# Three-sublayer decoder layer: every engine's order of steps written out as word lists instead of computed from slot tables, with three more waits

## What is computed

```
x = layernorm(x + attention(x))    # 16 heads of 16; causal; of each row only the 32 largest scores are kept,
                                   # softmax over them, times v, output projection
x = layernorm(x + experts(x))      # 8 experts: relu(proj_in[e] @ x) (256 -> 512), proj_out[e] @ h (512 -> 256),
                                   # weighted by gate[e], the sum of ctx where itok == e
x = layernorm(x + ffn(x))          # Hadamard rotation, 4-bit activations, ternary 256x256 weight
```

## Time and profile before

| | |
|---|---|
| three timed runs | 576.58, 575.6, 575.65 us (median 575.65) |
| profiled execution, first to last instruction | 574.0 us |
| busy: PE, DVE, ACT, POOL | 521.3, 457.4, 409.2, 346.6 us |
| mean granted clock of TensorE | 0.967 |
| bytes moved, mean | 24.08 MB, 42 GB/s |

### The profile page before, as it was taken

How to read it: one execution, slowest core, us unless ns; L and a number is a source line. 1 busy time by engine, 2 the same in 40 slices (tenths; PEclk the granted TensorE clock), 3 DMA queues, 4 the chain that set the end, 5 groups by cost and what they waited for, 6 DMA issues and landing times. The chain is left out here.

```text
span 574.0 us, 22290 instructions
## 1 busy us (share of the span) xinstructions
PE 521.3 (91%) x8116; PEld 443.4 (77%) x8116; DVE 457.4 (80%) x2846; ACT 409.2 (71%) x1018; POOL 346.6 (60%) x355
## 2 busy tenths in 40 slices
PE   5757659999999999999999999999999999999973
PEld 3535548888888888888888888888888888888851
DVE  2698988896988989998998889998999899504115
ACT  2888788776767687768866687768686878566641
POOL 1587485955547466755574556656565756476762
PEclk9888888999999999999999999999999999999995
DMA  7544440002000101100120102000200010000000
GB/s 228 174 150 148 126 157 18 3 2 59 3 24 18 23 3 38 40 3 21 41 58 2 23 11 67 3 22 3 76 4 22 2 39 3 1 2 19 2 14 24
DMA packets 23230, 24.08 MB, mean 42 GB/s; under 512 B 2129, under 2 KB 20049, under 8 KB 23121
## 3 DMA queue, kind: packets, MB, share of 16 engines
q1 hardware_dynamic: 23120, 22.65, 13.0%
HBM read 18.32 MB, written 2.10 MB: 36 GB/s over the span
## 5 line engine op out<-in xcount | busy, mean ns | idle before, releaser
L541 POOL TENSOR_TENSOR h_lo<-h_raw,h_hi 128x512 f16<-128x512 f32 x128 | 148.9, 1164 | 114.4 <-ACT h_raw L693 113.0
L895 PE MATMUL ps_o<-w_hi,h_lo 128*128 128x256 f16 x512 | 139.7, 273 | 3.5 <-POOL h_lo L541 3.5
L879 PE MATMUL ps_z<-x1t_hi,w_lo 128*128 128x256 f16 x512 | 140.0, 273 | 0.2 <-DVE x1t_lo L1043 0.2
L879 PE MATMUL ps_z<-x1t_lo,w_hi 128*128 128x256 f16 x512 | 139.7, 273 | 0.0
L879 PE MATMUL ps_z<-x1t_hi,w_hi 128*128 128x256 f16 x512 | 139.6, 273 | 0.0
L895 PE MATMUL ps_o<-w_hi,h_hi 128*128 128x256 f16 x512 | 139.6, 273 | 0.0
L895 PE MATMUL ps_o<-w_lo,h_hi 128*128 128x256 f16 x512 | 139.5, 273 | 0.0
L689 ACT ACTIVATE h_hi<-ps_z 128x512 f16<-128x512 f32 x128 | 76.2, 595 | 71.7 <-PE ps_z L879 71.6
L987 DVE MATCH_REPLACE8 taken<-next,taken 128x64 f32<-128x64 f32 (+4 forms) x480 | 110.7, 242 | 0.1
L562 POOL TENSOR_TENSOR acc<-go_sb,acc 128x512 f32<-128x512 f32 x55 | 70.0, 1273 | 34.3 <-ACT go_sb L703 34.2
L982 DVE MAX8 next<-taken 128x8 f32<-128x64 f32 (+4 forms) x480 | 85.5, 245 | 0.1
(11 more groups left out here) (142 smaller groups left out, 1037.3 us busy)
## 6 DMA issues: line engine op xcount, KB each, us to landing
w_raw<-in_w1t SPq DMA_DIRECT2D x8, 512.0 KB, 3.8
w_raw<-in_w2t SPq DMA_DIRECT2D x8, 512.0 KB, 3.7
v_pad<-v_sb SPq DMA_DIRECT2D x16, 136.0 KB, 2.7
xt_sb<-in_xt SPq DMA_DIRECT2D x8, 256.0 KB, 3.9
x_sb<-in_x SPq DMA_DIRECT2D x8, 256.0 KB, 3.1
xa_sb<-in_xt SPq DMA_DIRECT2D x7, 256.0 KB, 3.7
out<-out_sb SPq DMA_DIRECT2D x7, 256.0 KB, 3.8
ctx_sb<-in_ctx_w SPq DMA_DIRECT2D x8, 128.0 KB, 3.2
```

Of the source, the lines that this page charges most:

```text
L541: nc.gpsimd.tensor_tensor(h_lo[:, e % 2, 2 * z:2 * z + 2, :], h_raw[:, z, :, :], h_hi[:, e % 2, 2 * z:2 * z + 2, :], ALU.subtract)\
L879: last = pe.matmul(ps_z[z][:, d * UT:(d + 1) * UT], w[:, e, c, at:at + P], x[:, c, :], start=n == 0, stop=n == len(terms) - 1)
L895: last = pe.matmul(ps_o[e % 2][:, b * D:(b + 1) * D], h[:, e % 2, c, b * SEQ:(b + 1) * SEQ], w[:, e, c, :], start=n == 0, stop=n == len(te ...
```

## The change

The tables and the sort are gone. `ORDER` holds one string of step names for each engine; `name*3` stands for three steps in a row. The k-th time that a name stands in an engine's string, it is the k-th step of that name, by unit and then by the step's own numbers. `all_steps` lists what exists. All 477 PE steps, 429 DVE, 418 ACT, 280 POOL and 56 SP steps are the same as before. No instruction that computes or moves data is added, removed or altered.

```
-def build_schedule():
-    placed = []
-    def put(slot, engine, name, v, *args):
-        placed.append((slot, (engine, name, v, args)))
...
-    return [step for _, step in sorted(placed, key=lambda x: x[0])]
+ORDER = {
+    "pe": """
+        k q ffn_sum v scores*2 w_sum v w_sum k scores turn_probs q turn_probs k w_sum scores v turn_probs w_sum
+        v turn_probs scores attend turn_probs w_sum attend turn_probs k scores attend turn_probs*2 w_sum k v
+        attend turn_o w_sum out_proj q scores k turn_probs turn_x1 turn_probs L1 q L1 turn_probs L1*2 w_sum L1
...
+    "dve": """
+        gate_sums ffn_ternary first_max select*2 w_scale first_max select*5 keep w_scale select*7 first_max keep
...
+def all_steps():
...
+def build_schedule():
+    waiting = {}
+    for engine, name, v, *args in all_steps():
+        waiting.setdefault((engine, name), []).append((v, args))
+    waiting = {key: iter(sorted(steps)) for key, steps in waiting.items()}
+    placed = []
+    for engine, words in ORDER.items():
+        for word in words.split():
+            name, _, count = word.partition("*")
+            for _ in range(int(count or 1)):
+                v, args = next(waiting[engine, name])
+                placed.append((engine, name, v, args))
+    return placed
@@ exp on ACT
                     if n < TILES * UNITS - 1:
                         act.wait_ge(s_copied, n + 2)
+                    else:
+                        act.wait_ge(p_ready, n)
@@ x1t_high, x2t_high on ACT
                     act.wait_ge(ready, v + 1)
+                    if name == "x1t_high":
+                        wait(act, l1_done, RING_STEPS * v)
@@ gate_sums on DVE
                     dve.wait_ge(s_ctx, 32 * (v + 1))
+                    wait(dve, gate_ready, v)
```

More of the change, by code:

```diff
@@ L105, in expert_steps @@
     return steps + [("L2", EXPERTS - 1, 0), ("L2", EXPERTS - 1, 1)]
[L108 to L147, removed]
[3 rows of a table removed]
-    "gated_add": 2.5, "quantise": 85.5, "load_x": -14.5, "gate_scale": 48.75, "store": 102.75, "move_v": 10.25,
-    "q": -11.5, "load_ctx": 29.75, "gate_out": 0.5, "x1t_low": 43.75,
-}
@@ L155 @@
-FINAL = STEADY | {
-    "hadamard": 86.75, "copy_q4t": 99, "ffn": 130.5, "ffn_residual": 97.5, "ffn_scale": 97.25, "turn_q4": 99.75,
-    "to_q4": 86.75, "gate_out": -15, "quantise": 87.5, "out_proj": 59, "move_v": -4.25, "v": 98.5, "gate_sums": 31.5,
-    "turn_o": 38.25, "x2t_high": 80.25, "experts": 51.25, "keep": 4.5, "copy_probs": 2.5, "copy_q": -12,
-    "load_x": -18.25, "copy_k": -13, "rstd3": 97.5, "x1t_high": 52.25, "rstd2": 79, "load_xt": -25.25, "shift1": 2,
-    "turn_x1": 44, "x2t_low": 82.75, "normalise": 6.5, "x_plus_bo": 22, "x1t_low": 53.25, "shift0": 10, "attend": 5,
-    "gate_scale": 59, "h_low": -2.5, "turn_probs": 0.25, "turn_x2": 81.75, "select": 8, "spread_q": -11.75,
-    "copy_probs2": 4, "load_ctx": 26.5, "k": 75.25, "shift2": 2, "gated_add": 4, "copy_scores": -8.25, "relu": -2,
-    "pace": 1.25, "q": -9, "copy_v": 121.25, "scores": -5.5, "store": 105, "ln2_apply": 81.5, "shift3": 0.75,
-    "ln1_stats": 38, "rstd1": 39.5, "ln1_apply": 38.5, "turn_probs2": 8.25, "copy_ot": 36.75,
-}
@@ L220, in build_schedule @@
+def all_steps():
+    for v in range(UNITS):
+        for kind, e, z in expert_steps():
+            yield "pe", kind, v, e, z
+            if kind == "L1":
+                yield "act", "relu", v, e, z
+                yield "pool", "h_low", v, e, z
+            elif z == 1 and not (v == SPLIT and e == EXPERTS - 1):
+                yield "act", "gate_out", v, e
+                yield "pool", "gated_add", v, e
         for k in range(TILES):
-            tile = base + SLOTS // TILES * k + at[f"shift{k}"]
@@ L230, in build_schedule @@
-            put(base + at["spread_q"] + k, "pool", "spread_q", v, k)
+                yield engine, name, v, k
+            for half in range(2):
+                yield "pe", "turn_probs", v, k, half
+                yield "act", "copy_probs", v, k, half
         for b in range(UB):
-            put(base + at["gate_sums"] + b, "dve", "gate_sums", v, b)
+            yield "dve", "gate_sums", v, b
+            if v == SPLIT:
+                yield "dve", "gated_last", v, b
         for engine, name in UNIT_STEPS:
-            if v == 0 or (engine, name) not in AHEAD_STEPS:
-                put(base + at[name], engine, name, v)
+            yield engine, name, v
```

153 lines of the change are left out of this document (114 added, 39 removed), and 3 rows, old and new, of the table LAST.

## The result

| | before | after |
|---|---|---|
| timed runs | 575.6 to 576.58, median 575.64 us (4) | 565.56, 567.73, 569.25, 571.48, median 568.49 us (4) |
| ratio, with its 95% interval | | 0.9882 [0.9842, 0.9921] |
| profiled execution, span | 574.0 us | 563.7 us (its run: 565.56) |

The new order is 1.2% faster here; 570.0 was forecast. The four runs of the kernel after lie 6 us apart, and the profiled one is the fastest of them. So its rows alone would show too much. The same kernel was timed and profiled a second time, beside the experiments; there it is 0.7% faster (571.06 us).

A forecast was written before the change was run, and what follows sets the result against it. PE was taken as the bound from the first `L1`, before a fixed tail: 574.0 - 3.8 + 1.3 - 3.5 + 0.4 = 568.4 us span, plus 1.65 gives 570.0 us. Range 563 to 581; the forecast's own 566.5 to 573.

The forecast's parts named there:

- Projections, -3.8: `q2` and `k5` on PE fill the layernorm gap behind `out_proj0`, ahead of the first `L1`: 3.8 us gained.
- First `L1`, +1.3: `v0` ahead of the scores and changed DVE work start the first `L1` 1.3 us later, at 90.0; range -1 to +5.
- if the first `L1` lies beyond 93: Sign in the profile after: a first expert step on PE beyond 93 us would make the prediction wrong.
- Other marks: Profile signs: first scores near 18.3, `first_max` 20.4, `norm0.3` 76, PE busy over 98.5% from 100 to 500 us.
- `h_low`, -3.5: PE's waits for `h_low` between `L1` and `L2` vanish, since at least two steps separate them: 3.5 us, ends 2.0 and 3.5.
- Other waits, +0.4: PE waits 0.4 us more at `turn_x1(1)`; the remaining 4 us of waits arise anew. Ends -4 and +20.
- Three waits, 0: Added waits for `l1_done`, `gate_scale` and `keep` on ACT and DVE cost 0; bounds -0.1 and +1.5 us.
- tail, 0: The serial chain after the last `L2`, 17.6 us of layernorm, quantisation and ffn, keeps its order: 0 change.
- The rivals: The first: PE waits on ps_misc for `normalise` at 28 `attend`, 0.55 us each, 585 us; lower forms 577 to 581; chance 0.23.
- The late first scores are not made good: DVE keeps its 5.4 us of idle time and `L1` starts 4.4 us later still: 574.4 us; chance 0.12.
- the rule weighed: Idle gaps halve PE's clock; filling one spares `turn_x1(0)` and the first `L1` some 0.5 us, left out of the sum.
- `gate_sums`: On DVE, moving eight instructions away from POOL work saves 416 against 280 ns each by the shared-port rule; sum unchanged.

## Why the prediction was right, and where its sizes were off

The forecast was -5.6 us on the span, in four terms. The total held: 568.49 us and 571.06 us lie on either side of 570.0. That it came so near is in part luck. The forecast was -6.9 us behind the first `L1` and +1.3 ahead of it; the two profiles have -9.0 and -10.4 behind it, and -1.3 and +5.8 ahead.

*Projections, -3.8.* PE has 3.9 us less to do in the stretch in the first profile, and 5.5 less in the second (459.5 to 454.1). The difference is the clock again, 2.19 against 1.32 us for the first `L1` and 2.70 against 1.89 for `q3`; that the first agrees with 3.8 to 0.1 is luck, and some 1.4 us of the 5.5 are not accounted for. The term as the prediction put it, two projections that hide under the layernorm's 4.1 us, nearly holds at full clock, where they held `turn_x1(0)` 1.0 us. At the lower one `out_proj0` and `q2` took 7.5 us together instead of 4.0, and the first `L1` came late. The prediction priced that at 1 to 2 us "if one of them runs at the low clock" and left it out of the sum, while in the kernel timed again it happened. Undoing this part alone costs 5.2 us, the whole gain, though only some 3.9 of the 8.4 us in the stretch are the projections themselves. In the old lists the move was worth nothing: there the load for `q2` came too late, a condition that the prediction does not name and that the new list of SP meets.

*First `L1`, +1.3.* Measured -1.3 in the first profile and +5.8 in the second; by the spans of the timed runs +3 to +5 is usual (an estimate, as worked out above). The step that said `v0` delays the scores to 18.3 and `first_max` to 20.4 failed in its working: it took `v0` at 3.21 us and started it at 15.02. It took 1.99 us in both profiles and started at 13.34 in the first, because `q0` ran in 1.99 as well, and at 15.06 in the second. The scores came at 15.26 and 16.98, `first_max` at 17.37 and 19.07. The prediction also took `ffn_ternary` as worth nothing, since nothing waited for it in its old place; in the new list it stands ahead of the first `max`, and with the scores put first it alone held that `max` (17.58). DVE's own stretch was sized well as a whole: 76.0 - 20.4 = 55.6 us forecast, 56.12 and 57.86 measured, with 53.4 us of work (forecast 54.6) and 2.7 and 4.4 idle (forecast 1.0). What was missing is mainly the clock. The prediction read 0.86 in the earlier trace rows as a given of the kernel, when it moved between 0.91 and 0.79 in two executions of the new order, whose PE steps now lie on the path. One of its own marks says so: "if the first `L1` lies beyond 93" it would be wrong, and in one of the two profiles it lies at 94.47. Other marks held: PE busy 99.4% from 100 to 500 us, no wait for `normalise`, two projections in the gap, 0.5 us of waits for `h_low`. Those for the first scores, `first_max` and `norm0.3` (73.49 and 76.93 for 76) did not.

*`h_low`, -3.5.* Measured -3.0 by the list of waits (3.5 to 0.5); done alone, -2.9 in the stretch and some 2 in the time. The count behind it was off a little. Written out, 14 pairs of the old order have one expert step between, not 13. The new order isn't free of them either: four pairs have one, with three or more other steps beside it in three of them and two in the fourth.

*Other waits, +0.4.* Measured -2.0: idle time of PE went down by 5.0 us, 3.0 of which are `h_low`. The waits for `keep` (1.4), `quantise` (1.1) and `normalise` (0.7) of the earlier trace rows and of the same list went, a new one for `copy_probs` (0.9) came. The prediction had assumed that as much would arise anew, without a row for it.

*Three waits, 0, and tail, 0.* Both as put: 1.0000 [0.9983, 1.0016] and 17.3 us.

*The rivals.* PE did not wait for `normalise` in the kernel after. Its place was right, and with `normalise` two stages later its time is 581.9, between the 577 and the 585 that the prediction gave. Its form was off: seven waits of 1.4 us on the mean, not 28 of 0.55. Against it stood what the prediction said, two or more steps of PE behind most `attend`; with a margin of about 1 us the chance of 0.23 was a fair one. "The late first scores are not made good" (574.4) names a late start that did occur (94.47 in the second profile), with 4.4 us of DVE idle time in place of 5.4, but for another reason, mainly the clock.

Two points stay open. The stretch of the kernel after is 9 to 10 us shorter than before, and the two parts that were tried in the old order make 4.9 of it. The rest is presumably in the order of the later units, of which no part was isolated. And why one execution of the same lists gets 0.91 and another 0.79 was not found; `q0`, the second step, already differs (1.99 and 3.78 us, behind the same 0.93 us of idle time).

On the rule weighed (the Trainium skill, "TensorE: Matmul & The Clock Gate", section "HAM oscillation — how this bites in real kernels"): the two projections did spare `turn_x1(0)` (0.66 us instead of 1.09 for the same four matmuls), but not always the first `L1`. In the first profile it started behind 1.43 us of idle time, three of its matmuls took 0.27 to 0.28 us, and the last eight 0.42 each:

```profile
89.37 0.42 PE L918 MATMUL ps_z<-x1t_hi,w_hi 128*128 128x256 f16 x1
89.58 2.70 PE L792 MATMUL ps_misc<-xt_sb,wq_sb 128*128 128x256 f32 x8
```

From its first matmul to the next step it is 2.19 us, where 1.5 were needed before and 1.31 at full clock. In the second profile it started behind 1.12 us of idle time and took 1.32. That the rule would change little in the sum was right; where it mattered was not this one gap but the whole start.

On the other row weighed, `gate_sums`: the eight instructions were moved ahead of the first scores, but not to a time without POOL work. In the first profile two of the eight took 0.69 us instead of 0.29, beside `spread_q` on POOL (13.44 to 14.78). What the longer two-input instructions cost showed in `ffn_ternary`, 1.5 us in the second profile.
